# Edges of a graph layer grouped by 1024 instead of 512, in rows of ten slots, for buckets of 256 places

## The chip, the cores and the metric

The kernel runs on one core of one Trainium2 chip. The metric is device time in microseconds (us). Three runs of the kernel before gave 3584.20, 3589.17 and 3595.98 us, a median of 3589.17 us. An engine is named here as in the profile: PE is TensorE (PEld its weight loads), DVE is VectorE, ACT is ScalarE, POOL is GpSimd, SP is SyncE.

## The reference

There are 6250 nodes with 48 features and 206250 directed edges, sorted by `dst`, with 40 attributes and a distance each. Two layers follow one another:

```
# layer 0, self loops added; deg counts src
out0[col] += x[row] * rsqrt(deg[row]) * rsqrt(deg[col])
x = layernorm(x + out0)
# layer 1
gate = silu(edge_attr @ W1.T + b1) @ W2.T + b2 + sum(emb[z[src]] * (emb[z[dst]] @ adaptW.T))
cw   = 0.5*(cos(pi*dist/6)+1) if dist < 6 else 0
msg  = gate * x[dst] * (cw * mult[dst])
agg[src] += msg ;  tot[src] += mult[dst]
x = layernorm(x + layernorm_gamma_beta(x + agg / max(tot, 1e-8)))
```

The sum of layer 1 goes to `src`, while edges lie sorted by `dst`. So each message must be carried to another node, and this is what the change is about.

## The kernel before

Edges lie in 101 tiles (`NT`) of 16 columns (`G`) of 128. A node has a place: 62 nodes in each run of 64 places, so that 51 blocks (`NP2`) of 128 places hold them all.

**Setup (span start to about 408 us).** DVE and PE go over all tiles and count, with one-hot matrices, how many edges each node has (`deg`, L314) and how many each group of 512 edges has for each bucket of 128 places (`tot_bank`, L318). From these counts the first output row of each group and bucket is worked out (L504 to L526). SP clears the upper part of each bucket in the DRAM tensor `perm` with zeros (L235). A test (`near`, L540) chooses between the main path and a slow one for other graphs, in which nothing is routed.

**The tile loop (about 408 to 3216 us).** Each engine runs its own program over the tiles, through `over_tiles`: a list of steps, each with a lag in tiles, in the written order. Iteration T of an engine does each step for tile T minus its lag. The first and last iterations are unrolled, the middle is a loop of six tiles a turn.
- POOL gathers one row per edge from the table of nodes, 16 indirect DMAs a tile (L630), lag 0, and writes rows of messages to `perm` with four indirect DMAs a tile (L639), lag 5.
- PE: `layer1` and `layer2` are the two matrix products of the gate, `ranks` gives each edge its slot within its group and bucket, `rows_of_groups` the DRAM rows, `routes` moves messages into rows, `pick` fetches the data of `dst`, `total` sums layer 0. The order of an iteration is layer1(0), ranks(0), routes of groups 0 and 1 of the tile before, layer1(1), rows_of_groups, ranks(1), routes of groups 2 and 3, pick(0), layer2(0), pick(1), layer2(1), total.
- A group of four columns (512 edges) is routed into at most 128 rows of six slots (`R`). For slot j and column c a matmul with the one-hot `oh_r[:, c, j, :]` as weights adds 148 columns of `parts` (three bf16 parts of 49 values, and the low part of the place). That is 4 x 4 x 6 = 96 matmuls a tile (L734), in two banks of three slots, each emptied by ACT into `routed` (L779).
- DVE: an iteration copies the gather's indices (L849), makes the one-hots of buckets `oh_b` (L860), of `dst` `oh_t` (L863) and `oh_d` (L855), the steps `step_at` (L879), normalizes layer 0 every second tile (L918 to L948), takes the ranks out of PSUM (`spots`, L870), writes the rows' addresses (L888), makes the 16 one-hots `oh_r` of 768 elements (L899), and then runs `messages` (L973 to L1005): two halves, each a chain of seven operations in which ACT has a part.
- `oh_r` has one buffer. DVE may write group g of a tile when PE has routed group g of the tile before: `e.wait_ge(routing, 2 * (NG * (t - 1) + g + 1))`. `routes` waits for the whole of `messages` of its tile (`split_ok`).

**The bucket stage (about 3232 to 3502 us).** For each of 51 buckets SP loads 896 rows (7 a partition, three buffers), ACT copies the 42 keys, DVE compares them with a count (`onehot`, 128 x 42 elements, L1274), PE adds 42 matmuls (L1289), ACT empties the bank (L1250), DVE adds the three parts (L1265). Then comes the final normalization, to about 3595 us.

Of the kernel before, what the change touches and what calls it, by code (L numbers as in the profile page):

```python
# [28 lines left out]
NP2 = (NT + 2) // 2  # L29
NODE_ROWS = NP2 * P  # L30
U = 6
GR = 4
NG = G // GR
R = 6
# [3 lines left out]
CAP = 896  # L38
CLEAR = 640
AB = CAP // P  # L40
SPARE = NP2 * CAP
PERM = SPARE + NT * NG * P
EX = EM + 3 * C // 2
TW = C + EM + 1
MAGIC = 0x5F3759DF
DEEP = 1024
# [50 lines left out]
def build(nc, x, src, dst, edge_attr, edge_weight, node_type, node_vec, W1T, b1, W2T, b2,  # L97
# [4 lines left out]
    dst_pid = nc.dram_tensor("dst_pid", (P, K), I32).ap()  # L102
    far_rows = nc.dram_tensor("far_rows", (NODE_ROWS, TW), F32).ap()
# [3 lines left out]
    with ctx:  # L107
# [20 lines left out]
        pid_i = sb("pid_i", [P, K], I32)  # L128
        lo16 = sb("lo16", [P, K], BF16)
        hi16 = sb("hi16", [P, K], BF16)  # L130
        w16 = sb("w16", [P, K], BF16)
        weight = sb("weight", [P, K])
# [4 lines left out]
        rstart_t = sb("rstart_t", [NP2 + 1, NG, NT])  # L137
        delta_t = sb("delta_t", [NP2 + 1, NG, NT])
        rstart16 = sb("rstart16", [P, NP2, NG], BF16)
# [18 lines left out]
        with ExitStack() as ph:  # L158
            src_i = sb("src_i", [P, K], I32, ph)
# [15 lines left out]
            oh_hi = sb("oh_hi", [P, 2, NP2, G], BF16, ph)  # L175
# [8 lines left out]
            rows_i = sb("rows_i", [P, NG, NP2], I32, ph)  # L184
            rows_f = sb("rows_f", [P, NG, NP2], F32, ph)
            rows16 = sb("rows16", [P, NG, NP2], BF16, ph)
            goes_on = sb("goes_on", [P, NG, NP2], F32, ph)
            run_r = sb("run_r", [P, NG, NP2], F32, ph)
            first_b = sb("first_b", [P, NP2], F32, ph)
            spare_g = sb("spare_g", [P, NG], F32, ph)  # L190
            at_row = sb("at_row", [P, NG, NP2 + 1], F32, ph)
            rstart = sb("rstart", [P, NG, NP2 + 1], F32, ph)
            delta = sb("delta", [P, NG, NP2 + 1], F32, ph)
# [8 lines left out]
            turned_f = ps("turned_f", [NP2 + 1, 2, 512], F32, ph)  # L202
            tot = tot_bank[:, 0:NG * NP2].rearrange("p (g b) -> p g b", b=NP2)
            cum, all_rows, faults = (sums[:, k, 0:n] for k, n in enumerate((NP2, NP2, 1)))
# [3 lines left out]
             a_own, rows_set, rows_turned) = (  # L208
# [5 lines left out]
                                     "sq", "bad_ok", "fault_ok", "a_own", "rows_set", "rows_turned"))  # L214
            WB = -(-K // P)
            with nc.Block() as block:
                @block.sync
                def _(e):
# [10 lines left out]
                    for k in range(2):  # L229
                        e.dma_start(w1[RA * k:RA * (k + 1), C * k:C * (k + 1)], W1T).then_inc(wl, 16)  # L230
                        e.dma_start(w2[C * k:C * (k + 1), C * k:C * (k + 1)], W2T).then_inc(wl, 16)
                        e.dma_start(w2[2 * C:2 * C + 1, C * k:C * (k + 1)], b2).then_inc(wl, 16)
                    e.wait_ge(blank, 1)
                    for b in range(NP2):
                        e.dma_start(perm[CAP * b + CLEAR:CAP * (b + 1), :].rearrange("(p a) c -> p (a c)", p=P),  # L235
                                    zeros[:, :]).then_inc(filled, 16)
                    for k, (a, b) in enumerate(PARTS):
# [3 lines left out]
                                    tab[:, a:b, :]).then_inc(stored, 16)  # L241
                    e.wait_ge(wl, 16 * 12)
                    e.wait_ge(filled, 16 * NP2)
                    e.wait_ge(stored, 16 * len(PARTS))
# [56 lines left out]
                def _(e):  # L301
# [8 lines left out]
                    def count(i, s):  # L310
                        t = U * i + s
                        e.wait_ge(oh_ready, 2 * (t + 1))
                        for g in range(G):
                            e.matmul(deg[:, 0:NP2], oh_lo[:, s % 2, :, g], oh_hi[:, s % 2, :, g],  # L314
# [36 lines left out]
                def _(e):  # L351
# [15 lines left out]
                    e.iota(first_b[:, :], [[CAP, NP2]], base=0, channel_multiplier=0,  # L367
# [182 lines left out]
        with ExitStack() as ph:  # L550
# [50 lines left out]
            with nc.Block() as block:  # L601
# [46 lines left out]
                def _(e):  # L648
# [40 lines left out]
                    def ranks(m):  # L689
                        def step(i, s):  # L690
                            n = 2 * (U * i + s) + m
                            t = U * i + s
                            if m == 0:
                                e.wait_ge(ohb, t + 1)
# [761 lines left out]
```

## Time and profile before

| | |
|---|---|
| Profiled execution | 3596.59 us, span 3594.8 us |
| Median of three runs | 3589.17 us |
| PE busy | 2457.2 us, 68% |
| DVE busy | 2434.8 us, 68% |
| POOL busy | 2265.9 us, 63% |
| ACT busy | 1044.9 us, 29% |
| Mean granted PE clock | 0.832 |
| Bucket loads | 51 of 1554.0 KB, 8.0 us each from issue to landing |

No engine is busy for more than 68% of the span. So shares alone do not say what sets the time. One reads the stages one by one (the windows), and in each stage one tile in order of time (the timeline of an engine), looking for the wait that ends last.

### The profile page before, as it was taken

Reading aid. Unit: us, or ns where it says so; the run is one execution under the profiler, and the core shown is the slowest. Engines: PE = TensorE matmul, PEld = TensorE weight load, DVE = VectorE, ACT = ScalarE, POOL = GpSimd, SP = SyncE. Lnnn points to the kernel's source line nnn. Section 1 sums busy time; section 2 is a strip of 40 time slices with the busy share of each in tenths; the row PEclk is TensorE's granted clock in tenths of the full one; section 3 lists DMA queues with packets and bytes.
Section 4 is the critical chain, followed back from the end, with each engine's and each line's share of the span. In section 5 each row is a group of like instructions: output and inputs, shape, how many; then the busy total and the mean of one; then the engine's idle time right before and its main releaser. Section 6 shows DMA issues by size and latency. Waiting matters only on the chain. (4 is left out here: it accounts for less than half of the span.)

```text
span 3594.8 us, 69567 instructions
## 1 busy us (share of the span) xinstructions
PE 2457.2 (68%) x24398; PEld 2030.9 (56%) x24398; DVE 2434.8 (68%) x5609; ACT 1044.9 (29%) x2117; POOL 2265.9 (63%) x2116
## 2 busy tenths in 40 slices
PE   4899256677676767767677766767776767746760
PEld 3677145556555655656555655655555655646660
DVE  7755457777676776777776776777676777746654
ACT  0000123333333333333333333333333333421110
POOL 8700477777777777777777777777777777410002
PEclk9999987888788888888887877887887888868885
DMA  8000323333333333333333333333333333318871
GB/s 312 9 0 0 80 68 97 99 99 97 99 101 97 100 101 93 95 106 95 94 106 93 97 104 94 97 100 98 96 104 94 97 104 95 87 46 325 304 271 13
DMA packets 135012, 383.77 MB, mean 107 GB/s; under 512 B 53904, under 2 KB 53904, under 8 KB 128016
## 3 DMA queue, kind: packets, MB, share of 16 engines
q0 software_dynamic: 79200, 179.69, 18.7%
q1 hardware_dynamic: 53188, 198.17, 16.2%
q8 instruction: 218, 3.57, 0.4%
q10 hardware_dynamic: 2284, 1.33, 0.1%
q14 instruction: 122, 1.00, 0.1%
HBM read 258.83 MB, written 120.22 MB: 105 GB/s over the span
## 5 line engine op out<-in xcount | busy, mean ns | idle before, releaser
L630 POOL DMA_INDIRECT slot<-table,gidx x1616 | 1651.0, 1022 | 517.4 <-issue 485.0
L734 PEld LDWEIGHTS route<-parts,oh_r 128*128 128x128 bf16 x9696 | 810.1, 113 | 73.2 <-ACT routed L779 28.8
L734 PE MATMUL route<-parts,oh_r 128*128 128x148 bf16 x9696 | 828.8, 255 | 33.1 <-ACT routed L779 26.3
L779 ACT ACTIVATE routed<-route 128x444 bf16<-128x444 f32 x808 | 433.4, 541 | 770.4 <-PE route L734 763.7
L639 POOL DMA_INDIRECT perm<-routed,sidx x404 | 436.7, 1081 | 225.2 <-issue 207.1
L899 DVE TENSOR_SCALAR oh_r<-iota_r,spot 128x768 bf16<-128x768 f16 x1616 | 546.7, 413 | 5.2
L701 PE MATMUL rank<-oh_b,before 128*128 128x408 bf16 x202 | 87.7, 434 | 494.6 <-DVE oh_b L860 494.6
L870 DVE TENSOR_REDUCE spot<-rank 128x8 f32<-128x408 f32 x202 | 116.9, 579 | 407.9 <-PE rank L707 407.9
L701 PEld LDWEIGHTS rank<-oh_b,before 128*128 128x128 bf16 x202 | 20.2, 100 | 609.5 <-DVE oh_b L860 607.4
L668 PE MATMUL gate<-w,hid 97*128 97x96 f32 x1616 | 238.4, 294 | 161.2 <-DVE val L984 161.2
L828 ACT ACTIVATE parts<-val 128x392 bf16<-128x392 f32 x202 | 109.5, 542 | 746.3 <-DVE val L994 746.3
L668 PEld LDWEIGHTS gate<-w,hid 97*128 97x128 f32 x1616 | 209.4, 202 | 172.2 <-issue 172.2
L656 PE MATMUL phid<-attr,w 80*96 80x512 f32 x404 | 249.6, 704 | 57.9 <-issue 57.9
L1289 PE MATMUL acc<-rows,onehot 128*128 128x147 bf16 x2142 | 185.1, 259 | 107.1 <-issue 74.4
L1289 PEld LDWEIGHTS acc<-rows,onehot 128*128 128x128 bf16 x2142 | 180.5, 148 | 111.6 <-issue 111.6
L468 DVE TENSOR_TENSOR oh_lo<-number,lo 128x2048 bf16<-128x2048 bf16 x101 | 134.9, 1335 | 129.4 <-PE tot_bank L318 128.2
L684 PE MATMUL pwin<-win,oh_t 128*128 128x81 bf16 x4848 | 218.7, 200 | 0.0
L314 PEld LDWEIGHTS deg<-oh_hi,oh_lo 128*128 128x128 bf16 x1616 | 172.1, 148 | 61.9 <-issue 38.1
L749 PE MATMUL sums_f<-slot,oh_d 128*128 128x144 bf16 x1616 | 157.7, 267 | 66.5 <-DMA slot<-table,gidx 66.5
L1274 DVE TENSOR_TENSOR onehot<-count,mine 128x5376 bf16<-128x5376 bf16 x51 | 150.8, 2956 | 76.4 <-ACT mine L1256 76.3
L684 PEld LDWEIGHTS pwin<-win,oh_t 128*128 128x128 bf16 x4848 | 197.6, 97 | 2.6
L999 DVE TENSOR_TENSOR val<-val,parts 128x392 f32<-128x392 f32 x202 | 114.6, 567 | 124.1 <-ACT parts L828 124.1
(209 smaller groups left out, 3502.7 us busy)
## 6 DMA issues: line engine op xcount, KB each, us to landing
rows<-perm SPq DMA_DIRECT2D x51, 1554.0 KB, 8.0
oh_t<-dst_row SPq DMA_DIRECT2D x101, 512.0 KB
attr<-in_edge_attr SPq DMA_DIRECT2D x101, 320.0 KB
slot<-table,gidx POOLq DMA_INDIRECT x1616
perm<-zeros SPq DMA_DIRECT2D x51, 444.0 KB, 13.6
perm<-routed,sidx POOLq DMA_INDIRECT x404
table<-tab SPq DMA_DIRECT2D x3, 676.0 KB, 4.7
xin<-in_x SPq DMA_DIRECT2D x1, 1224.0 KB, 9.8
```

The source lines that it names most:

```text
L314: e.matmul(deg[:, 0:NP2], oh_lo[:, s % 2, :, g], oh_hi[:, s % 2, :, g], start=False, stop=False, skip_group_check=True)
L630: e.indirect_dma_start(out=slot[:, s, g, :], out_offset=None, in_=table0, in_offset=bass.IndirectOffsetOnAxis(ap=gidx[:, s, g:g + 1], axis ...
L639: e.indirect_dma_start(out=perm, out_offset=bass.IndirectOffsetOnAxis(ap=sidx[:, s % 2, g:g + 1], axis=0), in_=routed[:, s % 2, g, :], in_ ...
L656: e.matmul(phid[:, :], w1[:, :], attr[:, s % 2, 512 * m:512 * (m + 1)], start=True, stop=True).then_inc(hidden, 1)
L668: mm = e.matmul(gate[:, 2 * C * k:2 * C * (k + 1)], hid[:, P * c:P * (c + 1)], w2[:, :], start=True, stop=True)
L684: mm = e.matmul(at, oh_t[:, s % 2, m * HC + g, :], win[:, s, k, :], start=(k == 0), stop=(k == 2))
L734: mm = e.matmul(route[:, bank, RC * j:RC * (j + 1)], oh_r[:, GR * g + q, bank * R // 2 + j, :], parts[:, s % 2, GR * g + q, :], start=(q = ...
L749: mm = e.matmul(sums[:, 0:3 * C], oh_d[:, s % 2, :, g], rows[:, g, :], start=(g == 0), stop=(g == G - 1))
L779: e.activation(routed[:, s % 2, g, bank * ROW // 2:(bank + 1) * ROW // 2], route[:, bank, 0:ROW // 2], ACT.Copy).then_inc(rows_ok, 1)
L899: oh = e.tensor_scalar(oh_r[:, c], iota_r[:, :, :], spot[:, s % 2, c:c + 1], None, ALU.is_equal)
L1274: e.tensor_tensor(onehot[:, b % 2], count42[:, :, :], bc_mid(mine[:, b % 2], P), ALU.is_equal).then_inc(ohs, 1)
L1289: mm = e.matmul(acc[:, b % 2, 0:3 * MW], onehot[:, b % 2, :, c], rows[:, b % RS, c, 0:3 * MW], start=(c == 0), stop=(c == AB * R - 1))
```

## The change

Groups have eight columns (1024 edges, `GR` 8), so that a tile has two. A row has ten slots instead of six. A bucket has 256 places instead of 128, so that there are 26 (`NB`). A bucket has room for 1024 rows in `perm`. In detail:
- `routes` has 2 x 8 x 10 = 160 matmuls a tile, in four phases of 3, 3, 2 and 2 slots (`PHASES`), which take turns in two banks. There are two steps, `routes(0)` after `ranks` and `routes(1)` after `rows_of_groups`.
- `ranks` is one step a tile with 416 columns: one matmul with `lowered` (now minus 2048 on the diagonal, plus `before16`), seven with `ones16` (364, 312, ... 52 columns), one with `ident_r`.
- `oh_r` has ten times 128 elements a column. Its wait is `e.wait_ge(routing, NPH * (NG * (t - 1) + g + 1))`, with two groups.
- POOL has two scatters a tile, of rows of 2960 bytes instead of 1776.
- Indices and weights of a tile come by two DMAs of SP, out of DRAM tensors written in the setup. The index copy on DVE is gone, and lags on DVE are three less.
- The multiplier `mult[dst]` goes from `pwin` straight into `parts` by a second, small ACT instruction in `put_got`. The DVE copy L994 is gone, and products have 48 columns instead of 49.
- The counts are summed for pairs of blocks. The counting matmuls of a tile are 8 of 104 columns instead of 4 of 204.
- In the bucket stage, each of 26 loads (1024 rows, 8 a partition) serves two halves of 128 places. Each of the 51 halves goes over all 80 slots of a partition: `onehot` has 128 x 80 elements and there are 80 matmuls.

```diff
-GR = 4
+GR = 8
-R = 6
+R = 10
-CAP = 896
-CLEAR = 640
+CAP = 1024
+CLEAR = 768
+CLEAR_LAST = 256
+PHASES = ((0, 3), (3, 6), (6, 8), (8, 10))
...
+                    def ranks(i, s):
...
+                        e.matmul(at, lowered[:, :], mine, start=True, stop=False, skip_group_check=True)
+                        for k in range(1, GR):
+                            e.matmul(at[:, :, :, k:GR], ones16[:, :], mine[:, :, :, 0:GR - k], start=False,
+                                     stop=False, skip_group_check=True)
...
+                            for phase, (a, b) in enumerate(PHASES):
+                                n = NPH * (NG * t + g) + phase
+                                if since(i, s, 1) or g or phase >= 2:
+                                    e.wait_ge(rows_ok, n - 1)
+                                for j in range(a, b):
+                                    for q in range(GR):
+                                        mm = e.matmul(route[:, phase % 2, RC * (j - a):RC * (j - a + 1)],
+                                                      oh_r[:, GR * g + q, j, :], parts[:, s % 2, GR * g + q, :],
+                                                      start=(q == 0), stop=(q == GR - 1))
+                                mm.then_inc(routing, 1)
...
-                        over_tiles(e, NT, U, (layer1(0), 3), (ranks(0), 3), (routes(0, 2), 4), (layer1(1), 3),
-                                   (rows_of_groups, 3), (ranks(1), 3), (routes(2, NG), 4), (pick(0), 3),
-                                   (layer2(0), 3), (pick(1), 3), (layer2(1), 3), (total, 0))
+                        over_tiles(e, NT, U, (layer1(0), 3), (ranks, 3), (routes(0), 4), (layer1(1), 3),
+                                   (rows_of_groups, 3), (routes(1), 4), (pick(0), 3), (layer2(0), 3), (pick(1), 3),
+                                   (layer2(1), 3), (total, 0))
...
+                            e.activation(got[:, m].rearrange("p (b k) c -> p b k c", b=2), by_bank[:, :, :, 0:WX],
+                                         ACT.Copy)
...
+                            e.activation(of_mult, by_bank[:, :, :, WX:WW], ACT.Copy).then_inc(got_ok, 1)
...
                         for g in range(NG):
                             if since(i, s, 1):
-                                e.wait_ge(routing, 2 * (NG * (t - 1) + g + 1))
+                                e.wait_ge(routing, NPH * (NG * (t - 1) + g + 1))
...
+                        e.dma_start(gidx[:, s, :], src_pid[:, cols]).then_inc(index_in[s], 16)
+                        e.dma_start(weight[:, s, :], weights[:, cols]).then_inc(weight_in[s], 16)
...
-                            for c in range(AB * R):
-                                mm = e.matmul(acc[:, b % 2, 0:3 * MW], onehot[:, b % 2, :, c],
-                                              rows[:, b % RS, c, 0:3 * MW], start=(c == 0), stop=(c == AB * R - 1))
+                            for c in range(COLS):
+                                mm = e.matmul(acc[:, h % 2, 0:3 * MW], onehot[:, h % 2, :, c],
+                                              rows[:, s, c, 0:3 * MW], start=(c == 0), stop=(c == COLS - 1))
```

## Rows read from the trace of the kernel before

**Rows 1.** Windows of counting, tile loop, buckets: length, busy us by engine, clock, DMA.
```profile
180.00:270.00 90.00, 90.00 (x585) 67.47 (x584) 49.93 (x59) 0.00 (x0) 0.00 (x0) 1.00 0.00 0
...
1000.00:1500.00 500.00, 352.77 (x3676) 292.98 (x3676) 356.16 (x940) 180.17 (x362) 383.83 (x373) 0.83 0.35 98
...
3300.00:3400.00 100.00, 71.39 (x816) 69.41 (x815) 63.03 (x40) 10.73 (x39) 0.00 (x0) 0.83 0.80 301
```

**Rows 2.** Groups by line, POOL: busy us, mean ns, idle before, releasers.
```profile
L630 POOL DMA_INDIRECT slot<-table,gidx x1616 | 1651.0, 1022 | 517.4 <-issue 485.0 <-DVE gidx L849 25.1 <-ACT routed L779 6.1
...
L639 POOL DMA_INDIRECT perm<-routed,sidx x404 | 436.7, 1081 | 225.2 <-issue 207.1 <-ACT routed L779 17.5 <-DVE val L984 0.6
```

**Rows 3.** The line that starts DVE's iteration: ns least/median/most, first and last start.
```profile
L860 DVE TENSOR_TENSOR oh_b<-number,hi x101: 572/577/637, 461.6 to 3175.3; 128x816 bf16<-128x816 bf16 x101
```

**Rows 4.** Timeline of DVE, one tile without normalization: start, length, operation, idle before.
```profile
1511.09 0.58 DVE L860 TENSOR_TENSOR oh_b<-number,hi 128x816 bf16<-128x816 bf16 x1
1511.59 0.75 DVE L863 TENSOR_SCALAR oh_t<-oh_t,iota_p 128x2048 bf16<-128x2048 bf16 x1
1512.25 1.22 DVE L855 TENSOR_TENSOR oh_d<-number,w 128x2048 bf16<-128x2048 bf16 x1
...
1521.52 5.40 DVE L899 TENSOR_SCALAR oh_r<-iota_r,spot 128x768 bf16<-128x768 f16 x16
1526.84 0.27 DVE L973 COPY parts<-lo 128x16 bf16 x1
...
1536.61 0.58 DVE L860 TENSOR_TENSOR oh_b<-number,hi 128x816 bf16<-128x816 bf16 x1
```

**Rows 5.** Timeline of PE, the same tile and the start of the next.
```profile
1511.80 0.55 PE L701 MATMUL rank<-oh_b,before 128*128 128x408 bf16 x1
...
1513.49 4.33 PE L734 MATMUL route<-parts,oh_r 128*128 128x148 bf16 x48
1517.66 1.04 PE L656 MATMUL phid<-attr,w 80*96 80x512 f32 x2
1518.63 1.05 PE L717 MATMUL rank<-delta_t,step_at 52*128 x8
1519.62 0.35 PE L701 MATMUL rank<-oh_b,before 128*128 128x408 bf16 x1
...
1520.51 3.31 PE L734 MATMUL route<-parts,oh_r 128*128 128x148 bf16 x48
...
1537.24 0.52 PE L701 MATMUL rank<-oh_b,before 128*128 128x408 bf16 x1 [4.09 <-DVE oh_b L860]
...
1538.92 5.19 PE L734 MATMUL route<-parts,oh_r 128*128 128x148 bf16 x48
```

**Rows 6.** Waits between 1000 and 2500 us: total, times, longest.
```profile
DVE gidx L849 <- issue: 45.4, 9, 5.5
```

**Rows 7.** Timeline of PE, one tile of the counting.
```profile
345.42 1.66 PE L318 MATMUL tot_bank<-oh_hi,band 128*101 128x204 bf16 x4
346.89 1.79 PE L314 MATMUL deg<-oh_hi,oh_lo 128*128 128x51 bf16 x16
```

**Rows 8.** Groups by line: the copy that goes, a small ACT copy.
```profile
L994 DVE COPY val<-got 128x8 f32<-128x8 f32 x202 | 35.8, 177 | 30.1 <-DVE val L990 15.4
...
L803 ACT ACTIVATE win<-hm 128x48 bf16<-128x48 f32 x51 | 12.6, 246 | 14.1 <-DVE hm L957 14.1
```

**Rows 9.** Timeline of ACT: its part in the messages of a tile.
```profile
1504.93 0.69 ACT L817 ACTIVATE got<-pwin 128x648 f32<-128x648 f32 x1
```

**Rows 10.** Timeline of DVE, bucket stage.
```profile
3396.22 0.32 DVE L1265 TENSOR_REDUCE agg<-three 128x49 f32<-128x147 f32 x1 [0.96 <-ACT three L1250]
3396.46 2.95 DVE L1274 TENSOR_TENSOR onehot<-count,mine 128x5376 bf16<-128x5376 bf16 x1
```

**Rows 11.** Timeline of PE, bucket stage.
```profile
3399.51 2.94 PE L1289 MATMUL acc<-rows,onehot 128*128 128x147 bf16 x42 [0.60 <-issue]
```

**Rows 12.** Group of all routes, PE.
```profile
L734 PE MATMUL route<-parts,oh_r 128*128 128x148 bf16 x9696 | 828.8, 255 | 33.1 <-ACT routed L779 26.3 <-DVE parts L1005 6.8
```

More of the change, by code:

```diff
@@ L618, in _ @@
                     with when(e, 1):
-                        over_tiles(e, NT, U, (load, 0), (rows, 0))
+                        over_tiles(e, NT, U, (edges, 0), (load, 3), (rows, 3))
                 @block.gpsimd
@@ L769, in silu, with put_routed @@
                         return step
-                    def put_routed(g0, g1):
+                    def put_routed(g):
                         def step(i, s):
                             t = U * i + s
-                            if g0 == 0 and since(i, s, 2):
+                            if g == 0 and since(i, s, 2):
                                 e.wait_ge(scattered[s % 2], 16 * NG * pair_of(i, s))
-                            for g in range(g0, g1):
-                                for bank in range(2):
-                                    e.wait_ge(routing, 2 * NG * t + 2 * g + bank + 1)
-                                    e.activation(routed[:, s % 2, g, bank * ROW // 2:(bank + 1) * ROW // 2],
-                                                 route[:, bank, 0:ROW // 2], ACT.Copy).then_inc(rows_ok, 1)
+                            for phase, (a, b) in enumerate(PHASES):
+                                e.wait_ge(routing, NPH * (NG * t + g) + phase + 1)
+                                e.activation(routed[:, s % 2, g, RC * a:RC * b],
+                                             route[:, phase % 2, 0:RC * (b - a)], ACT.Copy).then_inc(rows_ok, 1)
                         return step
@@ L1029, in build @@
             to_i = sb("to_i", [P, K], I32, ph)
+            from_i = sb("from_i", [P, K], I32, ph)
+            weight = sb("weight_f", [P, K], F32, ph)
             to_f = sb("to_f", [P, K], F32, ph)
@@ L1235, in _ @@
                     with when(e, 1):
-                        for b in range(NP2):
+                        for b in range(NB):
                             s = b % RS
                             if b >= RS:
-                                e.wait_ge(used, b - RS + 1)
+                                e.wait_ge(used, 2 * (b - RS + 1))
                             e.dma_start(rows[:, s].rearrange("p a c -> p (a c)"),
```

392 lines of the change are left out of this document (208 added, 184 removed).

## The prediction

> **What bounds the kernel now.** I read the windows first [rows 1]. The tile loop takes about 2800 of 3595 us, so the change is decided there. In it PE, DVE and POOL are each busy for some 70 to 77% and none is full. The groups of POOL [rows 2] look like a bound: 2020 indirect DMAs take 1022 or 1081 ns each, and nearly all idle time between them is issue. Their busy time is (1651.0 + 436.7) / 2020 = 1.03 us each, with 0.30 us of issue 1.33, so 26.7 us for the 20 of a tile. The loop's period comes from the line that starts a DVE iteration [rows 3]: (3175.3 - 461.6) / 100 = 27.1 us a tile. So POOL is nearly full. But is it what the others wait for?
>
> The timelines of one tile answer this [rows 4, 5]. They show a ring of DVE and PE in which nothing waits for POOL:
> - DVE starts `oh_b` at 1511.09, PE starts the first ranks at 1511.80: 0.7 us.
> - ranks(0), to the first route at 1513.49: 1.7. Routes of two groups, to 1517.66: 4.2. layer1(1): 1.0. The eight small matmuls of rows_of_groups: 1.0. ranks(1), from 1519.62 to 1520.51: 0.9.
> - DVE takes the ranks, the addresses, and starts `oh_r` at 1521.52: 1.0. The 16 one-hots, to 1526.84: 5.3. Messages, to the next `oh_b` at 1536.61: 9.8.
>
> The sum is 25.5 us. A tile with normalization is about 1 us longer, and once in six tiles DVE stands still for 5 us at the loop's turn (45.4 us over 9 turns) [rows 6]. (3 x 25.5 + 3 x 26.6 + 5) / 6 = 26.9 us, near the 27.1 measured. So ring and POOL are almost level, and the ring is the one with the longer period. After the change POOL has 18 DMAs, near 24 us. What then counts is the ring alone.
>
> One more thing must be read in the rows of PE. Before ranks(0) PE had been idle for 4 us [rows 5], and the first matmuls after it run at half speed: ranks take 1.7 us against 0.9 later, and 48 routes take 4.33 or 5.19 against 3.31. The windows' granted clock of 0.83 [rows 1] is the mean of the two levels, 1.2 and 2.4 GHz.
>
> **The change, part by part: the ring of a tile.** Time 0 is the start of `oh_b`.
> - `oh_b` has 416 elements instead of 816. DVE's slope for this operation is (1.13 us - 0.50 us) / (2048 - 816), 0.51 ns an element (1.13 is the 1.22 of `oh_d` less the overlap of 0.09 that `oh_t` has with the next, 0.75 against 0.66) [rows 4], so 0.2 us goes: ranks start at 0.5.
> - Ranks: columns are 416 + 28/8 x 416 + 416 = 2288, against 1836 in one half now. At the low clock 1836 took 1.7 us, so 2.1: to 2.6. The second ranks (0.9) go.
> - routes(0), 80 matmuls. At the high clock 48 take 3.31, 69 ns each: 5.5 us. The low clock cost the two tiles shown 1.02 and 1.88 more, mean 1.45; since the ranks now use up some 0.4 us more of the low stretch, I take 1.2: to 9.3.
> - layer1(1) 1.0, to 10.3. rows_of_groups has half its matmuls, 0.5, to 10.8.
> - routes(1), 80 matmuls at the high clock, 5.5: to 16.3. ACT empties a bank in well under one phase (16 matmuls are 1.1 us), so no wait comes in between.
> - DVE has the ranks at 3.2, the row addresses at 11.0, and makes `oh_r` of group 0 until 14.7. For group 1 it must wait for the end of routes(1) of the tile before, 16.3. Now the same wait covers only the last four columns and is over before DVE gets there. This is the step that turns the order round: all 160 matmuls stand ahead of the second half of `oh_r`.
> - One `oh_r` of 1280 elements: now 5.32 / 16 = 0.333 us for 768. The slope of this kind of instruction is (0.66 - 0.33) / (2048 - 768), 0.25 ns (`oh_t` against `oh_r`) [rows 4], so 0.46 us. Eight are 3.7: to 20.0.
> - Messages: 9.8, less two copies with the idle time before them, (35.8 + 30.1) / 202 = 0.33 us each [rows 8], plus the small ACT instruction (0.25 by the nearest row [rows 8]) behind the 0.69 us copy of `got` [rows 9]. For the first half it hides behind the route wait; for the second it comes between two DVE steps that now follow without a gap, 0.2. Sum 9.3: to 29.3.
>
> So a plain tile takes 29.3 us instead of 25.5. In a normalizing tile the window steps of ACT hold back the addresses, group 0's one-hots end near 16.6, and only 0.3 more is lost: 29.6. Normalization itself (5 us) now hides behind the ranks and routes. With 5 us per six tiles: (3 x 29.3 + 3 x 29.6 + 5) / 6 = 30.3. My model gives 26.9 where 27.1 was measured, so I use the difference 3.2 to 3.4 and take +3.2 us x 100 = **+320 us**.
>
> What costs nothing: `step_at` and `spots` shrink beside PE's work. Two more DMAs on SP's queue wait for the gather and the messages of six tiles back, ahead of the attribute and `dst_row` loads, which are used two tiles later. The gather is queued two tiles ahead too, so their landing is hidden; if it were not, it would cost one landing a tile, and nothing in the ring waits for that. The scatters fall from four to two, 2.8 us of POOL, worth nothing once the ring is longer than POOL. If that cover fell (the ring under 24 us) POOL would be next.
>
> **Setup.** The four counting matmuls of 204 columns take 346.89 - 345.42 = 1.47 us, 0.37 each, and 16 of 51 take 1.6, 0.10 each [rows 7]: the time goes with the columns (1.7 ns each). Eight of 104 then take 8 x 0.19 = 1.5 us, +0.08 a tile, +8 us. The bound on the other side is that each keeps its 0.37: 1.47 x 101 = +148 us; the other end is 0. I take 8, since two rows of this stage agree on the slope. Four more DVE conversions after the count, fewer small steps: +4. The later start of clearing has 300 us of cover. **+12 us.**
>
> **End of the loop.** The last tile's routes are 64 matmuls more (4.4), messages 3 us later, two scatters fewer (-2.6): **+5 us**.
>
> **Bucket stage.** 42 matmuls take 2.94 us at the high clock [rows 11], so 80 take 5.6. A one-hot takes 2.86 us for 5376 elements (2.95 less the overlap [rows 10]), so 10240 take 5.4. They don't overlap fully: DVE starts the next one-hot only after ACT has emptied the bank (0.3) and it has added (0.32) [rows 10], 0.6 us after PE's end. Two halves take 5.6 + 0.6 + 5.5, so one takes 5.9. 51 x 5.9 = 300 us, and 17 us before the first matmul (a load of twice the bytes, a count of twice the elements, the first one-hot). Now the stage takes 270 us from its first load to its last matmul, paced by loads at 301 GB/s [rows 1]. **+47 us.** Bounds: +35 if DVE alone is the limit (5.65 each), +104 if PE stays at the mean of now (71.39 us / 816 = 87 ns [rows 1]). I take the middle value by rows, because in the counting stage PE is busy all the time and its granted clock is 1.00 [rows 1].
>
> **Sum.** 3596.6 (the profiled execution) + 320 + 12 + 5 + 47 = 3981. The median stands 7 us below that execution, so I predict **3974 us**.
>
> **Two rules of the Trainium skill.** The route rows show 69 ns for a weight load and matmul of 148 columns at 2.4 GHz [rows 5]. The Trainium skill (TensorE: Matmul & The Clock Gate, Back-to-back issue gap) gives about 81 ns for such a pair at 128 columns in a sustained stream; by it 160 routes would take 1.9 us more a tile, and the sum would be near 4165. The row is this kernel's own, so it decides. The same page (Loop structure matters more than you think) says that long waits between matmuls put PE at its low clock; the trace agrees (4.09 us idle, then 5.19 instead of 3.31).
>
> **Rivals.**
> - *PE stays low longer.* The mean of all routes now is 85 ns (828.8 us / 9696) [rows 12]. With that, 160 take 13.7 instead of the 12.2 above: +1.5 x 100, about 4125. For: the second tile shown recovers late. Against: only PE's stretch after the pause was slow, and the added work lies behind it. The skill's 81 ns would look the same in the total. 0.17.
> - *PE hardly goes low.* PE's share grows from 70%. Then ranks take 1.1 and routes(0) 5.5, the ring is 27.1 + 0.15 + 0.8 = 28.1, some +120 us for the loop, total about 3770. Against: PE still waits about 5 us for messages, as now. 0.14.
> - *POOL sets the pace (faster).* If the ring only fills what POOL leaves, the loop falls to 18/20 of it: 18 x 1.33 = 24.0 us, 100 x (24.0 - 27.1) = -310, plus 64 elsewhere: about 3345. It decides if the ring is shorter than 24 us. For: POOL has no gaps but issue. Against: the ring's pieces add up to the period without any wait for POOL. 0.05.
> - *The slow path for other graphs.* Not so: 1024 edges over 25 buckets in rows of ten make about 1024/10 + 0.45 x 26 = 114 rows of 128, and 202 groups fill about 910 of 1024 in a full bucket. 0.01.
>
> **How the numbers follow.** The forecast has 0.63. Its own range, with the bucket bounds and 1 us of ring either way, is 3880 to 4080. To hold 8 in 10 I go on toward both neighbours: 3750 to 4130. 0.3% is about what a measurement of this kernel can tell from no change (12 us over three runs). Faster: 0.05. Within 0.3%: 0.02. Slower: 0.93.
>
> **What would show it.** After the change `oh_b` should start every 30.3 us, with DVE waiting for a route before the ninth `oh_r` of a tile; POOL should have real gaps of some 6 us a tile; `oh_r` should take 0.46 us; the bucket stage should take some 317 us with PE near its high clock. If the period of `oh_b` is under 27 us, or POOL still has only issue between its DMAs, the ring argument is wrong.

## The result, and the profile after

The changed kernel takes 3878.51 us (3875.77 to 3879.59, four runs), the kernel before 3588.59 us beside it (3584.2 to 3595.98). The ratio is 1.0804, 95% interval 1.0786 to 1.0823: slower by 8%. The forecast was 3974 us, so sign and range were right and the size was 96 us too high. The nearest rival (PE hardly low, 3770) lies 108 us off on the other side: the truth is nearly in the middle of the two, so the number alone doesn't decide between them.

The windows come first, as before. A row has the stretch, its length, busy us (instructions) of PE, PE's weight loads, DVE, ACT and POOL, granted clock, DMA share, GB/s.

```profile
180.00:270.00 90.00, 90.00 (x693) 87.61 (x692) 49.80 (x58) 0.00 (x0) 0.00 (x0) 1.00 0.00 0
...
1000.00:1500.00 500.00, 396.35 (x4442) 338.65 (x4440) 345.98 (x810) 165.55 (x381) 323.08 (x313) 0.82 0.34 86
...
3600.00:3700.00 100.00, 100.00 (x1244) 100.00 (x1243) 90.61 (x31) 9.41 (x30) 0.00 (x0) 1.00 0.61 241
```

Against [rows 1], PE has more to do in the loop (396 us in 500, not 353) and POOL less (323, not 384). In the bucket stage PE has become full at the full clock, where it was busy for 71% at a clock of 0.83.

The first and last start of the line that begins a DVE iteration, and two groups of POOL (busy us, mean ns, idle before):

```profile
L899 DVE TENSOR_TENSOR oh_b<-number,bkt x101: 359/363/376, 468.2 to 3374.7; 128x416 bf16<-128x416 bf16 x101
```

```profile
L676 POOL DMA_INDIRECT slot<-table,gidx x1616 | 1620.2, 1003 | 515.5 <-issue 491.5 <-DMA gidx<-src_pid 23.4 <-ACT routed L817 0.6
...
L685 POOL DMA_INDIRECT perm<-routed,sidx x202 | 275.8, 1365 | 615.5 <-ACT routed L817 453.8 <-issue 161.7
```

The period is (3374.7 - 468.2) / 100 = 29.06 us, where it was 27.1 [rows 3]. Before, POOL had nearly only issue ahead of its DMAs [rows 2]. Now it waits 453.8 / 101 = 4.5 us a tile for ACT's routed rows. That is the mark that was forecast for a loop which POOL doesn't pace, though smaller than the 6 us given. Where the 283 us between the two spans (3877.8 and 3594.8) went:

| Stage | forecast | measured | from |
|---|---|---|---|
| Setup | +12 | +6.6 | first `oh_b` 461.6 to 468.2 |
| Tile loop | +320 | +192.8 | 2713.7 to 2906.5 us |
| End of the loop | +5 | +4.6 | the rest |
| Bucket stage | +47 | +79 | 270 to 348 us, first load to last matmul |

Two terms are wrong by much and partly cancel: the loop by -127, the buckets by +32.

Now one plain tile after the change, PE first, then DVE:

```profile
1637.65 0.53 PE L745 MATMUL rank<-oh_b,lowered 128*128 128x416 bf16 x1 [3.29 <-DVE oh_b L899]
1637.97 1.59 PE L747 MATMUL rank<-oh_b,ones 128*128 128x364 bf16 x7
...
1639.70 7.17 PE L774 MATMUL route<-parts,oh_r 128*128 128x148 bf16 x80
1646.71 1.04 PE L702 MATMUL phid<-attr,w 80*96 80x512 f32 x2
1647.68 0.60 PE L758 MATMUL rank<-delta_t,step_at 27*128 x4
1648.21 5.38 PE L774 MATMUL route<-parts,oh_r 128*128 128x148 bf16 x80
```

```profile
1637.23 0.36 DVE L899 TENSOR_TENSOR oh_b<-number,bkt 128x416 bf16<-128x416 bf16 x1
...
1648.39 0.22 DVE L923 TENSOR_SCALAR sidx<-rank,iota_p 128x2 int32<-128x2 f32 x1 [7.85 <-PE rank L758]
1648.63 3.79 DVE L934 TENSOR_SCALAR oh_r<-iota_r,spot 128x1280 bf16<-128x1280 f16 x8
1653.63 3.79 DVE L934 TENSOR_SCALAR oh_r<-iota_r,spot 128x1280 bf16<-128x1280 f16 x8 [1.21 <-PE route L774]
1657.34 0.19 DVE L1008 COPY parts<-key 128x16 bf16 x1
...
1666.50 0.36 DVE L899 TENSOR_TENSOR oh_b<-number,bkt 128x416 bf16<-128x416 bf16 x1
```

From `oh_b` at 1637.23 the steps stand at: ranks 0.4 (forecast 0.5), first route 2.5 (2.6), `layer1(1)` 9.5 (9.3), rows_of_groups 10.4 (10.3), second routes 11.0 (10.8), their end 16.2 (16.3), messages 20.1 (20.0), next `oh_b` 29.3 (29.3). The wait ahead of the ninth one-hot is there, 1.21 us. So for this tile the ring is right step by step. But this is the dearest of the plain tiles. The next rows are another one, with PE's first routes and a part of what it did at the tile's end:

```profile
1523.29 5.72 PE L774 MATMUL route<-parts,oh_r 128*128 128x148 bf16 x80
...
1541.16 1.99 PE L714 MATMUL gate<-w,hid 97*128 97x96 f32 x8 [2.45 <-DVE val L1019]
1542.94 2.13 PE L788 MATMUL sums_f<-slot,oh_d 128*128 128x144 bf16 x16
1544.86 1.95 PE L702 MATMUL phid<-attr,w 80*96 80x512 f32 x2
```

The same 80 matmuls take 5.72 us here, not 7.17, and this tile's period is 27.9 us. Both tiles run their ranks at the low level (granted clock 0.50). In the 7.17 us tile the low level goes on into the routes (0.73 from 1639.7 to 1646.8 us); here the routes have the high level almost at once (0.94 from 1523.3 to 1529.0). At this tile's end PE is low again (0.51): gates, sums and `layer1` take 1.99, 2.13 and 1.95 us, about twice their time at the high level (1.10, 1.2 and 1.04), but they stand beside DVE's messages and cost little.

The periods repeat every six tiles: 31.7, 28.8, 28.0, 29.3, 28.4, 27.9. The 31.7 has the loop's turn in it. They follow one thing only. Taken from the first start to the last, the first routes of these six tiles take 6.8, 6.4, 5.7, 6.9, 6.0 and 5.5 us, and the rest of each tile is 22.3 to 22.4 us (without the turn's 2.5), in all tiles that start between 1000 and 2500 us, plain or normalizing. So each us that the low level adds to the first routes is a us of the period.

The bucket stage, DVE and PE together, in order of time:

```profile
3598.46 5.49 DVE L1323 TENSOR_TENSOR onehot<-count,mine 128x10240 bf16<-128x10240 bf16 x1
3599.78 16.42 PE L1339 MATMUL acc<-rows,onehot 128*128 128x147 bf16 x202
...
3604.22 0.30 ACT L1294 ACTIVATE three<-acc 128x147 f32<-128x147 f32 x1 [5.79 <-PE acc L1339]
...
3604.55 0.33 DVE L1312 TENSOR_REDUCE agg<-three 128x49 f32<-128x147 f32 x1 [0.60 <-ACT three L1294]
3604.88 5.49 DVE L1323 TENSOR_TENSOR onehot<-count,mine 128x10240 bf16<-128x10240 bf16 x1
```

PE never stops, and a matmul takes 16.42 / 202 = 81 ns. Before it was 2.94 / 42 = 70 [rows 11], in which the end of the last matmul counts too: from start to start it was 66. DVE begins a one-hot every 6.4 us, and ACT and DVE wait for PE.

### The profile page after: what moved, and what is told of

It reads as the page before. It is cut to its first block and busy times, and to the rows that moved or that the text cites. A ratio compares the mean times of both kernels' runs of the same rounds, so it can differ in the third digit from the quotient of the medians.

```text
span 3877.8 us, 84862 instructions
## 1 busy us (share of the span) xinstructions
PE 2976.3 (77%) x32488; PEld 2622.9 (68%) x32489; DVE 2655.8 (68%) x5210; ACT 1044.1 (27%) x2421; POOL 2077.2 (54%) x1914
## 3 DMA queue, kind: packets, MB, share of 16 engines
q1 hardware_dynamic: 75652, 197.17, 16.3%
q0 software_dynamic: 69504, 164.37, 16.2%
## 5 line engine op out<-in xcount | busy, mean ns | idle before, releaser
L774 PE MATMUL route<-parts,oh_r 128*128 128x148 bf16 x16160 | 1194.5, 238 | 6.5 <-DVE parts L1038 6.5
L774 PEld LDWEIGHTS route<-parts,oh_r 128*128 128x128 bf16 x16160 | 1168.7, 103 | 27.6 <-issue 19.4
L934 DVE TENSOR_SCALAR oh_r<-iota_r,spot 128x1280 bf16<-128x1280 f16 x1616 | 770.8, 550 | 57.4 <-PE route L774 55.5
L817 ACT ACTIVATE routed<-route 128x444 bf16<-128x444 f32 (+1 forms) x808 | 387.3, 479 | 1019.5 <-PE route L774 1014.3
L685 POOL DMA_INDIRECT perm<-routed,sidx x202 | 275.8, 1365 | 615.5 <-ACT routed L817 453.8
L1339 PE MATMUL acc<-rows,onehot 128*128 128x147 bf16 x4080 | 331.1, 244 | 37.2 <-DVE onehot L1323 37.2
L1339 PEld LDWEIGHTS acc<-rows,onehot 128*128 128x128 bf16 x4080 | 330.8, 175 | 37.6 <-issue 37.5
L1323 DVE TENSOR_TENSOR onehot<-count,mine 128x10240 bf16<-128x10240 bf16 x51 | 280.0, 5493 | 6.6 <-ACT mine L1302 6.4
L788 PEld LDWEIGHTS sums_f<-slot,oh_d 128*128 128x128 bf16 x1616 | 187.9, 165 | 67.1 <-DMA slot<-table,gidx 40.0
L731 PE MATMUL pwin<-win,oh_t 128*128 128x80 bf16 (+1 forms) x4848 | 220.5, 201 | 3.2
L731 PEld LDWEIGHTS pwin<-win,oh_t 128*128 128x128 bf16 x4848 | 199.2, 98 | 19.5 <-ACT parts L865 19.4
```

The costliest lines, as they stand in the source:

```text
L685: e.indirect_dma_start(out=perm, out_offset=bass.IndirectOffsetOnAxis(ap=sidx[:, s % 2, g:g + 1], axis=0), in_=routed[:, s % 2, g, :], in_ ...
L731: mm = e.matmul(pwin[:, g // 4, first:first + n], oh_t[:, s % 2, m * HC + g, :], win[:, s, AT[k]:AT[k] + n], start=(k == 0), stop=(k == 2) ...
L774: mm = e.matmul(route[:, phase % 2, RC * (j - a):RC * (j - a + 1)], oh_r[:, GR * g + q, j, :], parts[:, s % 2, GR * g + q, :], start=(q == ...
L788: mm = e.matmul(sums[:, 0:3 * C], oh_d[:, s % 2, :, g], rows[:, g, :], start=(g == 0), stop=(g == G - 1))
L817: e.activation(routed[:, s % 2, g, RC * a:RC * b], route[:, phase % 2, 0:RC * (b - a)], ACT.Copy).then_inc(rows_ok, 1)
L934: oh = e.tensor_scalar(oh_r[:, c], iota_r[:, :, :], spot[:, s % 2, c:c + 1], None, ALU.is_equal)
```

## The experiments

The theory: the loop is a ring of DVE and PE, the routes stand on it, and POOL has slack. The rivals: POOL's DMAs set the pace; or the work itself, not its order, is the price. For the bucket stage the question was why a matmul takes 80 ns.

**A difference between chips comes first**, as these numbers can't be read without it. The kernel before took 3589 to 3594 us in the first comparison and on two of the chips used for the experiments, and 4718 to 4739 us on three others, called the slow chips here. There every kernel's tile loop is slow and the setup 17 to 41 us longer, and the bucket stage is not (a matmul of the changed kernel's stage takes 81 ns there too). A kernel is compared only with the kernel before on its own chip. The first four kernels below ran on slow chips alone, and the changed kernel without an edit never ran on one.

*Two gathers fewer in the kernel before.* POOL issues 14 gathers a tile; two sixteenths of the gathered rows are zero and left out.

```diff
-                        for g in range(G):
+                        for g in range(G - 2):
```

> The kernel before, without the gathers of two of its 16 columns (their slots hold zeros): POOL has 18 indirect DMAs a tile, as many as after the change. Ring theory: the period stays at what DVE and PE give, 26.9 of 27.1 us: -10 to -30 us, some 3565. POOL theory: -270, some 3320.

Measured: 4404.9 us against 4738.52, ratio 0.930 (0.9213 to 0.9386).

On record were some 3565 us for the ring and 3320 for POOL, for a kernel before of 3589. The 334 us less lie nearer to POOL's theory. But the chip was a slow one, so this isn't a test of it.

*Two gathers more in the changed kernel*, into a buffer that nothing reads.

```diff
+                        for g in range(2):
+                            e.indirect_dma_start(out=spare[:, s, g, :], out_offset=None, in_=table0,
...
```

> The kernel after, with two more gathers a tile into a spare tile that nothing reads, so that POOL has 20 indirect DMAs a tile again. Ring theory (DVE and PE set a period of 29.06 us, POOL needs 20 x 1.33 = 26.7): no change, 3878 us within 15. POOL theory (POOL sets the pace): +2 x 1.33 x 101 = +270, some 4150. If the two are coupled through the late scatter, something between, up to +60.

Measured: 5093.93 us, ratio 1.0754 (1.0654 to 1.0854). It was run again on another chip:

> The changed kernel with two more gathers in each tile, into a buffer that nothing reads: POOL issues 18 gathers and 2 scatters. Ring theory (the loop's pace is the ring of ranks, place numbers, one-hots and routes between TensorE and VectorE; POOL waits some 5 us of each tile for the routed rows): two more gathers cost POOL 2.5 us of those 5, the period stays 29.1 to 29.4 us, the kernel 3878 to 3905 us. POOL theory (POOL's calls set the pace, or what holds the routed rows is their landing): +2.5 us a tile, 3878 + 101 x 2.5 = 4131 us.

It met a second slow one, where the kernel before took 4718.38 us: 5095.49 us, ratio 1.0784 (1.0698 to 1.0871). The period was 40.8 us on both.

*Fewer routing matmuls in the changed kernel:* three of the eight one-hots of each group are left out.

```diff
-                                    for q in range(GR):
+                                    for q in range(5):
```

> The kernel after, with only five of the eight columns of a group routed: 100 route matmuls a tile instead of 160, all else the same (three columns of each group are left out of the sums). Ring theory: a plain tile loses the wait before its ninth one-hot and gets 3.4 us shorter, a normalizing one 2.0: -2.7 x 101 = -270, some 3610, POOL then at its limit in part. A theory in which DVE's own longer one-hots (7.5 us instead of 5.3) are the cause and PE is not on the path: no change beyond 1%.

Measured: 4662.49 us, ratio 0.9843 (0.9747 to 0.994). Again:

> The changed kernel with routing matmuls left out: five of the eight one-hots of each group are multiplied, so a tile has 100 routing matmuls in the place of 160 (the sums are then wrong for the edges left out). Ring theory: the 60 matmuls at 65 ns stand on the path of the tile almost whole, 3.9 us less, of which 0.5 to 1 may be lost to ScalarE's copies of each phase: period 25.2 to 26.5 us, kernel 3480 to 3610 us. POOL theory: no change beyond 0.5 us a tile, 3830 to 3880 us.

On the second slow chip 4661.69 us, ratio 0.9877 (0.9792 to 0.9961). The period was 36.7 and 36.6 us.

*One-hots of the routes in three buffers.*

```diff
-            oh_r = sb("oh_r", [P, G, R, P], BF16, ph)
+            oh_r = sb("oh_r", [P, BUFS * GR, R, P], BF16, ph)
...
-                                e.wait_ge(routing, NPH * (NG * (t - 1) + g + 1))
+                                e.wait_ge(routing, NPH * (NG * t + g - BUFS + 1))
```

> The kernel after, with three buffers of eight one-hots instead of two, so that the second half of a tile's one-hots waits for the first half of the tile before, not for all of it. Ring theory as I predicted it (that wait is the step that turns the order round): only the plain tiles have the wait (1.2 us by the trace), so -0.6 x 101 = -60, some 3815; nearly all of the longer ring stays, since the row addresses come only after routes(0). If the wait were the whole cause of the loss: -200. If it only moves to another wait: 0.

Measured: 4886.02 us, ratio 1.0312 (1.0238 to 1.0386). The period was 38.9 us.

The expectations had been made for a loop of 27 to 29 us a tile, and the loop there is another one. Beside the 38.9 us of this kernel, two gathers more and 60 matmuls fewer each move the period by some 2 us, so there both seem to stand on the path; neither theory said that. (The fitting comparison would be the changed kernel itself on such a chip, which is missing.) The waits of the kernel with 14 gathers, from 1000 to 2500 us, in total, times and longest ("remote" is a semaphore raised by something that the trace doesn't name):

```profile
POOL perm L639 <- ACT routed L779: 487.4, 43, 17.8
ACT routed L779 <- remote: 422.4, 74, 15.6
...
PEld route L734 <- issue: 153.1, 145, 10.6
```

In the kernel before on a fast chip no wait of the same stretch is put down to "remote", and none for issue is longer than the 5.5 us of [rows 6]. The queue of the indirect DMAs isn't slower by packet. Packets, MB and share of 16 engines' span, first the kernel before on the fast chip, then the one with 14 gathers:

```profile
q0 software_dynamic: 79200, 179.69, 18.7%
```

```profile
q0 software_dynamic: 72736, 168.92, 13.9%
```

A packet takes 0.187 x 16 x 3594.8 / 79200 = 136 ns and 0.139 x 16 x 4404.7 / 72736 = 135 ns. A gather call of POOL is no longer either (1017 ns, 1022 in [rows 2]); a scatter call is 0.1 us longer (1185 ns for 1081). So neither the calls nor the packets make up the time. The engines are released late, PE even inside a group of matmuls, and what releases them isn't in the trace. It isn't the landing of the scatters alone: in the kernel with three buffers ACT's second copy of a group needs only PE's 48th matmul. PE had done 61 of them by 1535.1 us, and ACT copied at 1540.4. The cause stays open, and those runs decide nothing about the ring on the fast chips.

*The changed kernel once more,* on another chip.

> The changed kernel as it is, as the yardstick for the other kernel of this chip. Expected 3878 us and a tile loop with a period of 29.1 us, with the kernel before at 3589. If this chip is one on which the kernel before takes some 4740 us, as in the four runs before this one, then the changed kernel is expected near 4840 us (1.02 times the one before), for there the tile loops are held by something else than in the two traces of the comparison: the waits of ScalarE and VectorE for scatters that the trace puts down to no instruction.

Measured: 3878.58 us against 3594.3, ratio 1.0794 (1.0774 to 1.0813). So the result repeats.

*The bucket stage's one-hot in two blocks of 40 places,* on that chip. DVE makes as many elements and PE does as many matmuls. Only the distance between weight columns changes, from 160 to 80 bytes.

```diff
-            onehot = sb("onehot", [P, 2, P, COLS], BF16, ph)
+            onehot = sb("onehot", [P, 2, NK, P, CB], BF16, ph)
...
-                                mm = e.matmul(acc[:, h % 2, 0:3 * MW], onehot[:, h % 2, :, c],
+                                mm = e.matmul(acc[:, h % 2, 0:3 * MW], onehot[:, h % 2, c // CB, :, c % CB],
```

> Bucket stage of the changed kernel alone: each half's one-hot is written as two blocks of 40 places, so that a weight column lies 80 bytes from the next and not 160; VectorE writes the same 128x10x80 elements, TensorE does the same matmuls. Theory A (the stride at which TensorE loads the weights sets the 80 ns between matmuls): spacing 65 to 70 ns, VectorE's 5.5 + 0.3 us per half becomes the bound, the stage goes from 348 to 310-320 us and the kernel to 3840-3850 us, ratio to the changed kernel 0.990. Theory B (a stream of matmuls kept up this long runs at 80 ns whatever the stride, from the back-to-back rate or from reading the rows): spacing stays 80 ns, stage 348 us, kernel 3878. Theory C (the strided write costs VectorE more): the one-hot goes over 5.5 us and the stage gets longer.

Measured: 3851.03 us (3847.19 to 3852.23) against 3878.58 (3876.15 to 3880.67) for the changed kernel on the same chip: 27.6 us less. The groups of the stage, first the changed kernel, then this one (busy us, mean ns, idle before):

```profile
L1339 PEld LDWEIGHTS acc<-rows,onehot 128*128 128x128 bf16 x4080 | 330.8, 175 | 37.6 <-issue 37.5
L1323 DVE TENSOR_TENSOR onehot<-count,mine 128x10240 bf16<-128x10240 bf16 x51 | 280.0, 5493 | 6.6 <-ACT mine L1302 6.4
```

```profile
L1343 PEld LDWEIGHTS acc<-rows,onehot 128*128 128x128 bf16 x4080 | 274.5, 144 | 66.3 <-issue 66.3
L1326 DVE TENSOR_TENSOR onehot<-count,mine 128x5120 bf16<-128x5120 bf16 x102 | 283.5, 2822 | 9.0 <-ACT mine L1304 8.6
```

And its timeline of PE, two halves of a bucket:

```profile
3602.89 5.45 PE L1343 MATMUL acc<-rows,onehot 128*128 128x147 bf16 x80 [0.32 <-issue]
3608.95 5.45 PE L1343 MATMUL acc<-rows,onehot 128*128 128x147 bf16 x80 [0.60 <-issue]
```

A matmul takes 5.45 / 80 = 68 ns, a weight load 144 ns and not 175. So theory A holds: the distance between weight columns set the 80 ns. Theory B would have left it there. By the single records the matmuls of one half start 66 ns apart, as in the kernel before (84 bytes); with the 160 bytes it is 80. DVE is the bound now (5.56 + 0.34 us a half) and PE has gaps, which is why 27.6 us came back and not the 53 that 4080 matmuls at 13 ns would give. The time is 1 us above the expected range. Theory C is out as well: the one-hot takes 2 x 2.8 us where it took 5.5. The changed kernel's stage also begins at 80 ns: its first 46 matmuls, at the low level, start 123 ns apart in the single records, and from the next few on they start 80 ns apart. So a long stream isn't needed for it. The 123 ns are the same with 80 and 84 bytes: at the low level the distance cost nothing.

*The loop in another order.* Three buffers of one-hots. PE takes the group rows ahead of all routes, and window and gate between the two halves of the routes. DVE makes places and scatter rows ahead of the normalization, and ACT copies half a group at a time.

```diff
-                        over_tiles(e, NT, U, (layer1(0), 3), (ranks, 3), (routes(0), 4), (layer1(1), 3),
-                                   (rows_of_groups, 3), (routes(1), 4), (pick(0), 3), (layer2(0), 3), (pick(1), 3),
+                        over_tiles(e, NT, U, (layer1(0), 3), (ranks, 3), (rows_of_groups, 3), (routes(0), 4),
+                                   (layer1(1), 3), (pick(0), 3), (layer2(0), 3), (routes(1), 4), (pick(1), 3),
```

> The changed kernel with the same work in another order. One-hots of the routes in three buffers of eight chunks and not two, so VectorE writes the next tile's first half while TensorE still routes; TensorE takes the ranks and the group rows first, and the gate and window matmuls between the two halves of the routes; VectorE makes places and scatter rows ahead of the normalization; ScalarE copies the routed rows in halves of a group. Ring theory: the two waits that make the period (VectorE's one-hots for the routes of the tile before, TensorE's routes of the second group for the one-hots) go off the path, and the period falls to the busiest engine with its gaps: TensorE is busy 23 us a tile, POOL's calls take 23.3, so 25 to 27.5 us, kernel 3470 to 3720 us. Work theory (the extra work itself, not its order, is the price): the period stays within 0.5 us of 29.1, kernel 3830 to 3930 us.

Measured on the second slow chip: 4869.48 us, ratio 1.0305 (1.0222 to 1.0387), period 38.7 us, as with three buffers alone.

*The same, with the bucket one-hot in five blocks of 16* (weight columns 32 bytes apart, and PE waits for each block by itself).

> The order of the kernel above together with the bucket stage's one-hot in blocks: five blocks of 16 places, weight columns 32 bytes apart, TensorE waiting for each block alone. Expected: the gain of the reordered kernel plus 28 to 40 us of the bucket stage (28 was measured for two blocks of 40, where VectorE's 5.9 us per half had become the bound; a start at the first block can take away only the pipeline's own gaps). Kernel 3440 to 3690 us; if it is under 3590 it beats the kernel before as well. A stride of 32 bytes could cost TensorE or VectorE something that 80 bytes did not: then the stage is over 320 us.

On the same slow chip it took 4828.23 us, ratio 1.0216 (1.0131 to 1.0301). Again:

> The same kernel as before (other order in the loop, one-hot of the bucket stage in blocks), for the two chips of the earlier runs held every tile loop at 36 to 41 us a tile whatever its order, and say nothing on the ring. On a chip where the kernel before takes 3590 us: ring theory 25 to 27.5 us a tile and 310 to 320 us for the bucket stage, 3440 to 3690 us in all, under the kernel before if the period is below 26.5; work theory 28.6 to 29.5 us a tile, 3800 to 3890 us. The run tells the two apart by the period alone; what the bucket stage brings is known from the kernel with two blocks of 40.

On a third slow chip 4831.09 us, ratio 1.0202 (1.0128 to 1.0276). The last run:

> The last kernel once more, as its run also fell on a chip where the kernel before takes 4730 us. Where the kernel before takes 3590 us, as said: ring theory 25 to 27.5 us a tile, 3440 to 3690 us in all; work theory 28.6 to 29.5 us a tile, 3800 to 3890 us. Where the kernel before takes 4730 us: 4830 us again, and the order of the loop stays untried.

Measured there: 3786.4 us (3784.58 to 3786.94) against 3588.7, ratio 1.0541 (1.0519 to 1.0562). It doesn't beat the kernel before. Of the 92 us against the changed kernel 59 are the loop's and some 33 come behind it. Both theories named a range that the mean period missed: 28.5 us a tile, hardly under the 28.6 of the work theory and far from 27.5. The waits from 1000 to 2500 us, first of the changed kernel, then of this one, with the start of `oh_b` between them:

```profile
DVE sidx L923 <- PE rank L758: 185.8, 26, 7.9
...
PE rank L745 <- DVE oh_b L899: 160.3, 51, 3.6
...
DVE oh_r L934 <- PE route L774: 29.3, 26, 1.2
...
DVE prod L1013 <- ACT parts L865: 10.6, 51, 0.2
```

```profile
L901 DVE TENSOR_TENSOR oh_b<-number,bkt x101: 361/368/377, 468.4 to 3316.1; 128x416 bf16<-128x416 bf16 x101
```

```profile
PE rank L746 <- DVE oh_b L901: 216.9, 53, 5.5
...
DVE oh_r L936 <- PE route L775: 77.6, 27, 3.7
...
DVE sidx L925 <- PE rank L759: 72.0, 53, 1.4
...
DVE prod L1015 <- ACT parts L866: 70.9, 53, 2.0
```

The wait that was aimed at (DVE's for the group rows) fell by 114 us. The one for buffers grew by 48, PE's for `oh_b` by 57, and DVE's for ACT's `parts` by 60, as ACT's steps were moved too. The messages of both halves still end a tile on DVE, and PE has done all its own work well before they are through. So it stands idle longer, and pays for it after. PE, in two tiles of this kernel, and the group of all routes, first of the changed kernel, then of this one:

```profile
1619.05 8.16 PE L775 MATMUL route<-parts,oh_r 128*128 128x148 bf16 x80
...
1629.79 5.37 PE L775 MATMUL route<-parts,oh_r 128*128 128x148 bf16 x80
...
1642.42 0.53 PE L746 MATMUL rank<-oh_b,lowered 128*128 128x416 bf16 x1 [3.49 <-DVE oh_b L901]
```

```profile
L774 PE MATMUL route<-parts,oh_r 128*128 128x148 bf16 x16160 | 1194.5, 238 | 6.5 <-DVE parts L1038 6.5
```

```profile
L775 PE MATMUL route<-parts,oh_r 128*128 128x148 bf16 x16160 | 1296.9, 250 | 5.0 <-DVE parts L1040 5.0
```

The same 16160 matmuls take 102 us more, 1.0 us a tile: the first half of the routes now takes 6.4 to 7.9 us from first start to last, mostly at the low level, the second 5.1 as before.

The mean hides what the order did. DVE, a plain tile, and the point in the next one, with normalization, at which it waits for ACT's window:

```profile
1614.56 0.37 DVE L901 TENSOR_TENSOR oh_b<-number,bkt 128x416 bf16<-128x416 bf16 x1
...
1641.99 0.37 DVE L901 TENSOR_TENSOR oh_b<-number,bkt 128x416 bf16<-128x416 bf16 x1
...
1653.60 0.21 DVE L994 TENSOR_TENSOR hm<-hm,win 128x48 f32<-128x48 f32 x1 [1.94 <-ACT win L843]
```

Means of the tiles that start between 1000 and 2500 us, without the loop's turn:

| us | before | changed | other order |
|---|---|---|---|
| Plain tile | 25.8 | 28.7 | 26.6 |
| Normalizing tile | 26.7 | 28.5 | 29.4 |
| Tile without its first routes | | 22.3 to 22.4 | 19.4 to 19.6 plain, 21.6 to 22.1 normalizing |

Plain tiles are 25.9 to 27.4 us, inside the range of the ring theory. Normalizing ones got longer than in the changed kernel. In them DVE's one-hots wait for the window, and ACT makes the window behind its copies of the first routes. These routes now begin later in the tile, 4.5 us after `oh_b` and not 2.5, and run slower. So the first one-hot begins 12.4 us after `oh_b` (at 1654.35), where it was 11.3 in the changed kernel. So order and buffers took 2.9 us out of a plain tile's rest and some 0.5 out of a normalizing one's, 1.7 in the mean; the low level of the first routes took 1.0 of it back, and 0.6 to 0.7 is left. The order and the buffers were not tried apart on a fast chip.

This kernel also ran on both kinds of chip. Its gather calls take 1022 ns on the slow one and 1065 on the fast one, its scatter calls 991 and 994, its packets 144 and 146. Only the loop differs, 38.7 us a tile for 28.5.

## Why the forecast was right, and where it was off

**Right: the ring, and POOL's slack, as the trace shows them.** The period rose though POOL lost two DMAs a tile, POOL got waits of 4.5 us a tile, every step listed of the plain tile is within 0.2 us, and the first routes pass into the period one for one. POOL's rival is out by this, not by an experiment: the two kernels with other numbers of gathers ran only where another thing rules. That the order of the ring costs time was tried once on a fast chip. Of the 2.9 us by which plain tiles had grown (25.8 to 28.7) the other order took back 2.1, with the same matmuls; in the mean of all tiles it took back only 0.6. How much the 64 added matmuls alone cost there wasn't measured.

**Luck in the number.** The loop came 127 us under its term and the buckets 32 over, so the sum is nearer than its terms. The rival's price has a slip too: its ring of 28.1 us less the 27.1 measured, as the forecast counts its own, gives +100 and not +120 us, so some 3750.

**Off: three sizes in the loop.** The step "+3.2 us x 100" measured +1.93.
- *The routes.* The forecast had 5.5 + 1.2 us for the first 80 and 5.5 for the second. To the start of the next step the first take 6.3 in the mean of the six tiles (5.6 to 7.0) and the second 5.2: 0.4 and 0.3 us a tile. The mean by the group is 1194.5 / 16160 = 74 ns against 85 before [rows 12]; the forecast's 12.2 us a tile is 76. The rate of 69 ns had been read from 48 matmuls, with the last one's end in it, and 80 of them show 5.38 / 80 = 67. I had given the routes the same low stretch each time; it reaches into them by 0.4 to 1.8 us.
- *The loop's turn.* I kept 5 us for it. It took 2.5, as the row below shows beside [rows 6]: 0.4 us a tile. Why the turn got shorter wasn't tried.
- *Normalizing tiles.* I had 0.3 us more for them than for plain ones. They have nothing more: DVE's 16 one-hots run without a break behind the window steps, and the rest of the tile is the same 22.3 to 22.4 us. 0.15 us a tile.

These make 1.25 us, and the period is 29.06 where 30.3 was forecast.

```profile
DVE oh_b L899 <- issue: 22.2, 9, 2.7
```

The rivals on PE's clock were both on the right quantity and both too strong. "Low longer" put 85 ns on every route, "hardly low" 5.5 us on the first half. The counting of the ring with one typical tile hid that the end of the low stretch moves from tile to tile.

**Wrong: PE's rate in the bucket stage.** This term was mis-sized. The step that failed is "42 matmuls take 2.94 us, so 80 take 5.6". They take 6.4, as the columns of the one-hot's weights had moved from 84 to 160 bytes apart, a thing of the layout that the count of matmuls doesn't show. With 5.45 the stage cost 28 us less. The bounds of +35 to +104 held the +79; my choice of +47 within them was 32 us too low. The routes, with weights side by side, stay at 67 ns.

The Trainium skill (TensorE: Matmul & The Clock Gate, Back-to-back issue gap) gives about 81 ns for a weight load and matmul of 128 columns in a sustained stream. The 16.42 us for 202 looks like it, but the trace agrees only for that layout (and has 147 columns in the matmul): 80 in a row take 67 ns each in the routes and 68 in the blocks of 40.

**Small terms.** Setup took 6.6 and not 12 us: the row below has eight counting matmuls of 104 columns in 352.85 - 351.32 = 1.53 us, against 1.47 for the four of 204, some 6 us in 101 tiles. So the slope by columns was right, and the four conversions cost next to nothing. The loads of indices and weights are hidden: POOL waits 23.4 us for `gidx` over the whole run.

```profile
351.32 1.70 PE L339 MATMUL tot_bank<-oh_hi,band 128*101 128x104 bf16 x8
352.85 1.80 PE L335 MATMUL deg<-oh_hi,oh_lo 128*128 128x51 bf16 x16
```

## What to carry to other kernels

In a ring of two engines forecast the period from several neighbouring tiles, not from one: the same 80 matmuls cost 5.4 us or 8.1 by what PE did just before. When a tile is made wider, look at the distance between weight columns as well as at the number of matmuls; cutting a one-hot in blocks gave the rate back, and here cost the engine that writes it 1% (5.56 us for 5.49). When a loop has two kinds of tile, read the periods of each: another order took 2.1 us off the one kind and added 0.9 to the other, and the mean showed 0.6. And a wait taken out of a ring can come back as idle time ahead of the matmuls that start the next tile, and with it the low clock: here 1.0 us a tile of the 1.7 that had been won.

## What the hardware showed that was not expected

- At the high level, with weight columns 160 bytes apart, matmuls of 147 columns start 80 ns apart and a weight load takes 175 ns (medians of the single records). With 84 bytes it is 66 and 141, with 80 bytes 66 and 143, with 32 bytes 67 and 144. At the low level it is 123 ns with 160, 84 and 80 bytes alike.
- A loop's turn on DVE cost 5.0 us a time in one kernel and 2.5 in another with the same number of iterations.
- On three chips the tile loop took 35 to 41 us a tile in all kernels tried, with POOL's gather calls and DMA packets as long as ever (1.02 us, 135 ns) and waits that end by nothing in the trace. The bucket stage was no slower. Ratios between kernels changed there as well: the reordered kernel with blocks was at 1.020 to 1.022 of the kernel before, and at 1.054 on a fast chip.
